# Feed-forward rows turned by VectorE and DMA instead of TensorE, and two steps of the attention rows moved to GpSimd

## What is computed

```python
x = X
q, k, v = xpos(norm(x) @ W_Q), xpos(norm(x) @ W_K, down), norm(x) @ W_V
p = softmax(q @ k.T) * 0.9 ** abs(n - m)          # n, m: row and key
x = x + p @ v
def fp4(x):                                       # blocks of 16 along the row
    scale = maximum(max(abs(block)) / 6, 1e-12)
    return grid(block / scale) * scale            # 0, .5, 1, 1.5, 2, 3, 4, 6
z = fp4(norm(x))
h = silu(z @ fp4(w_gate).T) * (z @ fp4(w_up).T)   # 704 wide
out = x + fp4(h) @ fp4(w_down).T
```

## Time and profile before

| | |
|---|---|
| median of 3 runs | 2549.67 us (2548.38 to 2549.73) |
| span of the profiled execution | 2546.6 us |
| PE, PEld busy | 2518.4, 2290.0 us |
| DVE, ACT, POOL busy | 2140.9, 1489.8, 1816.8 us |
| granted TensorE clock | 0.999 of 2.4 GHz |
| DMA, mean over the span | 80 GB/s |

### The profile page before, as it was taken

One profiled execution on the slowest core, in us unless ns is written; L12 is line 12 of the kernel. 1 busy time (PEld: TensorE's weight loads), 2 busy tenths in 40 slices (PEclk: granted clock), 3 DMA queues, 4 the chain that ended last, 5 costly groups with the idle time before them and its releaser, 6 DMA issues.

```text
span 2546.6 us, 51904 instructions
## 1 busy us (share of the span) xinstructions
PE 2518.4 (99%) x16160; PEld 2290.0 (90%) x16160; DVE 2140.9 (84%) x4759; ACT 1489.8 (59%) x2966; POOL 1816.8 (71%) x1929
## 2 busy tenths in 40 slices
PE   8999999999999999999999999999999999999997
PEld 7888879999999999999999999999999999999996
DVE  8999878888878888888888888888888888888886
ACT  5766565656555655566565656565556655555654
POOL 6999956667767676667766776677666776677665
PEclk9999999999999999999999999999999999999999
DMA  8878511122111311131112111131113111211110
GB/s 285 302 271 299 186 50 30 34 86 66 38 40 45 107 37 42 34 106 42 42 34 91 62 38 40 45 107 39 42 34 106 41 42 34 95 58 38 40 38 22
DMA packets 163473, 203.27 MB, mean 80 GB/s; under 512 B 15184, under 2 KB 116752, under 8 KB 163216
## 3 DMA queue, kind: packets, MB, share of 16 engines
q1 hardware_dynamic: 163216, 200.01, 24.1%
HBM read 103.42 MB, written 77.59 MB: 71 GB/s over the span
## 4 chain that ended last, share of the span: by engine, by line
PE 85%; POOL 0%; DVE 0%; issue 0%; ACT 0%; POOLq 0%
PE score L516 27%; PE acc L655 19%; PE ring L516 19%; PE acc L516 9%; PE ring L622 6%; PE ring L675 3%; PE acc L697 1%; PE ring L613 1%; DVE hT L1226 0%; POOL probs L998 0%; ACT probs L823 0%; ACT hT L793 0%; POOL h_buf L1019 0%; POOL xv L1004 0%; POOL h_buf L1013 0%
## 5 line engine op out<-in xcount | busy, mean ns | idle before, releaser
L516 PE MATMUL score<-keys,q_st 128*128 128x512 f32 x3072 | 733.7, 394 | 3.0 <-ACT probs L823 2.6
L516 PEld LDWEIGHTS score<-keys,q_st 128*128 128x128 f32 x3072 | 567.0, 188 | 117.8 <-issue 3.0
L998 POOL TENSOR_TENSOR probs<-probs,decay 128x512 f32<-128x512 f32 (+3 forms) x416 | 450.7, 1097 | 197.5 <-ACT probs L823 197.5
L655 PE MATMUL acc<-vals,pT 128*128 128x256 f32 x3984 | 554.6, 286 | 0.8 <-DVE pT L1226 0.8
L516 PE MATMUL ring<-w_gu,xqT 128*128 128x512 f32 (+1 forms) x2304 | 509.1, 374 | 0.0
L655 PEld LDWEIGHTS acc<-vals,pT 128*128 128x128 f32 x3984 | 498.1, 189 | 7.3 <-DVE pT L1226 2.0
L516 PEld LDWEIGHTS ring<-w_gu,xqT 128*128 128x128 f32 x2304 | 419.0, 188 | 63.6 <-DVE xqT L1226 0.4
L793 ACT ACTIVATE xqT<-ring 128x256 fp32r<-128x256 f32 x128 | 49.3, 385 | 706.9 <-PE ring L613 706.9
L1239 DVE TENSOR_REDUCE smax<-score 128x1 f32<-128x1024 f32 x256 | 312.8, 1222 | 95.6 <-PE score L516 94.1
L1226 DVE TENSOR_TENSOR pT<-ring,pT 128x512 fp32r<-128x512 f32 (+3 forms) x432 | 248.7, 600 | 66.7 <-ACT pT L793 65.5
L1004 POOL TENSOR_TENSOR xv<-xv,xe 128x256 f32<-128x256 f32 x128 | 94.4, 737 | 269.1 <-DVE xv L1079 269.1
(11 more groups left out here) (133 smaller groups left out, 4470.0 us busy)
## 6 DMA issues: line engine op xcount, KB each, us to landing
k_dram<-keys SPq DMA_DIRECT2D x56, 512.0 KB, 4.5
keys<-k_dram SPq DMA_DIRECT2D x56, 512.0 KB, 7.3
edge<-vals SPq DMA_DIRECT2D x288, 64.0 KB, 2.1
q_raw<-q_dram SPq DMA_DIRECT2D x129, 128.0 KB, 2.6
x_in<-X SPq DMA_DIRECT2D x32, 512.0 KB, 4.5
q_dram<-q_stage SPq DMA_DIRECT2D x32, 512.0 KB, 5.4
x_res<-X SPq DMA_DIRECT2D x128, 128.0 KB, 2.1
out<-x_res SPq DMA_DIRECT2D x128, 128.0 KB, 1.7
```

What stands on the lines that cost most here:

```text
L516: mm = pe.matmul(dst, stat(a, k), mov(m, k), start=i == 0, stop=ends and i == n - 1)
L655: mm = pe.matmul(pv_out, pT[g % 2][:, a, j * P:(j + 1) * P], edge[places[m]][:] if kb in edges else vals[m][:, kb, :], start=i == 0, stop= ...
L998: op = pool.tensor_tensor(probs[:, k0:k1], probs[:, k0:k1], decay[:, off + k0:off + k1], ALU.mult)
```

## The change

- TensorE's `h_transposed` is gone, with its two slots of the ring. In its place VectorE turns the 24 blocks of 32x32 of each quarter (`h_turned_blocks`, one `dve.transpose` over 128x768), for tile s-4, after the lower halves of the pieces. SP writes the turned tile to DRAM in one DMA, waits for it, and reads it back in four DMAs of 32 partitions each into `hqT` (`rows_turned`), which puts the quarters in their places. The next step ScalarE copies the upper half of all 768 columns from `hqT`, after pieces 0 and 1, and VectorE makes the lower half (`h_lower`) after its pieces 0 and 1 and ahead of the second maximum. Both now read SBUF.
- `hq` is one buffer instead of two; the other half holds the turned rows. So GpSimd's rounding of h waits for VectorE's transpose of the tile before.
- In the chain of xv GpSimd makes the block scales (`x_block_scales`, after all decay products) and, after `values`, the factor `rstd2 * xrs` and the product with xv (`x_normalised`). VectorE keeps the maxima, the reciprocal and the rounding. VectorE waits twice more for GpSimd (`x_scaled`, `x_normed`).
- Tile 0's blocks are cut 4, 4 instead of 2, 3, 3. With two pieces, GpSimd's `rstd` follows both decay products.
- On SP, `rows_turned` stands after `load_q`, ahead of values, edges, store and residual load.

```diff
@@ groups
-    size = CT if 0 < t < T - 1 else CT - 1
+    size = CT if t < T - 1 else CT - 1
@@ plan_slots
-            for h in range(2):
-                if g == min(max(len(gs) - LATER, 0) + h, max(len(gs), 1) - 1) and has(s - LAG):
-                    take("hT", s - LAG, h)
@@ buffers
-        hq = [hq_buf[:, i * FT:(i + 1) * FT] for i in range(2)]
+        hq, h_turn = (hq_buf[:, i * FT:(i + 1) * FT] for i in range(2))
+        hqT = [sb(f"hqT{i}", [P, CT, HK * QUAD]) for i in range(2)]
+        h_dram = nc.dram_tensor("h_dram", (2, P, CT, HK * QUAD), F32, kind="Internal").ap()
@@ SyncE
+            def rows_turned(j, t):
+
+                g, i = j * T + t, t % 2
+                sp.wait_ge(h_turned, g + 1)
+                passed()
+                if t > 1 or not isinstance(j, int) or j:
+                    sp.wait_ge(h_split, g - 1)
+                    passed()
+                sp.dma_start(h_dram[i], h_turn.rearrange("p (c r) -> p c r", c=CT)).then_inc(turn_out, 16)
+                sp.wait_ge(turn_out, (g + 1) * 16)
+                for c in range(CT):
+                    sp.dma_start(hqT[i][c * QUAD:(c + 1) * QUAD, :, :], h_dram[i, :, c, :].rearrange("(a i) r -> i a r", a=CT)).then_inc(hqT_back[i], 16)
@@ step
+                if s >= TURNED or not is_first:
+                    rows_turned(j, s - TURNED)
@@ ScalarE, h_transposed, now after pieces 0 and 1
-                    for h, n in enumerate((CT, HK - CT)):
-                        upper(hT[0][:, h * CT:h * CT + n, :].rearrange("p k t -> p (k t)"),
-                              bank(at, "hT", t, h)[:, 0:n * P], at, "hT", t, h)
+                    act.wait_ge(hqT_back[t % 2], halves(at, t) * CT * 16)
+                    if has(at, t - 1):
+                        act.wait_ge(dn_done, tile(at, t))
+                    act.activation(chunks(hT[0][:]), quads(hqT[t % 2][:]), ACT.Copy).then_inc(h_upper, 1)
@@ GpSimd
+            def x_block_scales(at, t):
+                if has(at, t):
+                    g = tile(at, t)
+                    pool.wait_ge(x_maxed, g + 1)
+                    pool.sem_inc(pool_passed, 1)
+                    pool.tensor_scalar(xs[:], xam[:], rstd6[:, 0:1], 1e-12, ALU.mult, ALU.max).then_inc(x_scaled, 1)
+
+            def x_normalised(at, t):
+                if has(at, t):
+                    g = tile(at, t)
+                    pool.wait_ge(ln2_rstd, g + 1)
+                    pool.wait_ge(x_inverse, g + 1)
+                    pool.tensor_tensor(xrs[:], xrs[:], rstd2[:, 0:1].to_broadcast([P, XB]), ALU.mult).then_inc(x_factor, 1)
+                    pool.wait_ge(x_factor, g + 1)
+                    pool.tensor_tensor(blocks(xv[:]), blocks(xv[:]), spread(xrs[:], XB), ALU.mult).then_inc(x_normed, 1)
@@ step
+                x_block_scales(at, s - 1)
                 for h in values_at(at, s):
                     values(at, h)
+                x_normalised(at, s - 1)
                 x_quantised(at, s - 1)
@@ VectorE
+            def h_turned_blocks(at, t):
+                if has(at, t):
+                    dve.wait_ge(hq_ready, tile(at, t) + 1)
+                    if has(at, t - 1):
+                        dve.wait_ge(turn_out, tile(at, t) * 16)
+                    dve.transpose(h_turn.rearrange("p (c k j) -> p k c j", c=CT, j=QUAD), hq.rearrange("p (k c i) -> p k c i", c=CT, i=QUAD)).then_inc(h_turned, 1)
+
+            def h_lower(at, t):
+                if has(at, t):
+                    dve.wait_ge(h_upper, tile(at, t) + 1)
+                    dve.tensor_tensor(chunks(hT[1][:]), quads(hqT[t % 2][:]), chunks(hT[0][:]).bitcast(F32), ALU.subtract).then_inc(h_split, 1)
@@ step
                 attend(at, s - 1, range(min(n, 2)))
+                h_lower(at, s - LAG)
                 maxima(at, s, 1)
...
                 attend(at, s - 1, range(2, n))
-                for h in range(2):
-                    h_transposed(at, s - LAG, h)
+                h_turned_blocks(at, s - TURNED)
```

More of the change, by code:

```diff
@@ L46 @@
 RING = 3
-XR, LAG, LATER = 8, 5, 3
+XR, LAG, TURNED = 8, 5, 4
+QUAD = 32
 W_SLOTS = 3
@@ L502, in _ @@
                 step(B - 1, s, False, False)
-            for t in range(T - LAG, T):
-                store(B - 1, t)
+            for s in range(T, T + LAG):
+                if s - TURNED < T:
+                    rows_turned(B - 1, s - TURNED)
+                store(B - 1, s - LAG)
             for i in range(XR):
@@ L687, in down @@
                 if has(at, t):
-                    copied(at, "hT", t, 1)
+                    pe.wait_ge(h_split, tile(at, t) + 1)
                     if t == 0 and at[2] is first_plan:
@@ L1306, in x_levels @@
                     return
-                then, wait, count = chain(xq_step, (tile(at, t) + 1) * NSTEP_XQ - 3)
-                wait()
-                dve.wait_ge(ln2_rstd, tile(at, t) + 1)
-                then(dve.scalar_tensor_tensor(blocks(xv[:]), blocks(xv[:]), rstd2[:, 0:1], spread(xrs[:], XB), ALU.mult, ALU.mult))
+                then, wait, count = chain(xq_step, tile(at, t) * NSTEP_XQ)
                 meanwhile(0)
-                wait()
+                dve.wait_ge(x_normed, tile(at, t) + 1)
                 levels(then, wait, xv[:], xe[:], xg_ready, meanwhile)
-                assert count() == 3
+                assert count() == NSTEP_XQ
             def h_made(at, t, p):
```

59 lines of the change are left out of this document (23 added, 36 removed).

## The result

The changed kernel takes **2696.2 us** (median; 2694.1 to 2700.0), the kernel before 2549.6 beside it: a ratio of 1.058 (95% interval 1.056 to 1.059), 146.5 us more. I had forecast 2609, at most 2662: the sign was right, the size was not.

What follows compares the result with a forecast made beforehand. TensorE was taken as the bound, by only 0.4 us. Per batch -6.9 + 6.4 + 5.0 = +4.5, eight times 36, plus 14 and 9 = +59: 2609 us; own range 2570 to 2650, wider range 2490 to 2662.

Steps and rivals of the forecast that it cites:

- rounding of h: VectorE's rounding of h, held at its old length of 900 ns beside an idle GpSimd; no cost in the sum.
- six transposes: Six transposes a pass leave TensorE, taken as 0.65 us a pass, 83 us if all of it arrived.
- x part: Scale and product of xv in GpSimd's queue make the next first maximum late in some passes: 5.0 us a batch.
- collision of `h_lower` (c): `h_lower` waits for GpSimd's subtraction ahead of the second maximum: 0.33 us, or 0.7 in some passes; 6.4 us a batch.
- borders: At batch borders the turned rows' DMAs queue behind the next batch's keys: 2 us, 7 times, 14 us.
- end: At the kernel's end the DMA round trip stands open once, about 11 us for 2 of the old path: 9 us.
- signs named ahead: TensorE idle 0.5 to 2 us a pass before piece 2, `h_lower` above 1.2 us, VectorE waiting on GpSimd, late first maximum.
- The transpose, 0.9: VectorE's block transpose of 128x768, not in the trace, taken as 0.9 us; bounds near 0.5 and 1.8.
- Rival 4: VectorE's transpose takes 1.8 us, ahead of `var`: 65 us more, 2674 us; chance 0.09.
- rival 1: TensorE keeps the bound and the gain arrives, c near 0, late passes covered: 2505 to 2520 us; chance 0.33.
- Rival 2: Gain and losses cancel within 0.2%, c near 0, late passes as worked out: 2549 us; chance 0.07.
- Rival 5: The DMA round trip is over 1 us too slow in every pass: 2700 us; chance 0.08.

Runs made afterwards that it cites:

- mixed: turn_wait with `h_lower` ahead of the first maximum; TensorE transposes h for one tile in 16 and the last four; tile 0 in three pieces: 2534.2 us.
- One_input: The changed kernel with `h_lower` as an instruction with one input of the same size, the lower half of h left out of the result: 2615.2 us.
- x_only: The kernel before with only the scale and product of the attention rows moved to GpSimd; hT still goes through TensorE: 2574.3 us.
- turn_only: The changed kernel with the scale and product of the attention rows back on VectorE, all else kept: 2620.6 us.
- turn_wait: turn_only with GpSimd's decay products waiting until VectorE has rounded h: 2599.3 us.
- x_early_wait: x_early with GpSimd's decay products also waiting until VectorE has rounded h: 2646.4 us.
- x_early: The changed kernel with GpSimd's scale directly behind `rstd` and its product with xv ahead of the values' work: 2673.4 us.

## Why the prediction was right in sign and wrong in size

**The step that failed.** The sum took the terms of a pass one by one and held everything the change doesn't touch at its old length and place. The largest term so missed is the rounding of h, put at nothing: it went from 900 to 1552 ns, and keeping GpSimd from it gives back 41 us. By the experiments and the ledger, what was forecast and what was found, in us of the kernel:

| term | forecast | found |
|---|---|---|
| six transposes | -83 | -46 |
| rounding of h beside the decays | 0 | 41 |
| x part, on top of the turned rows | 40 | 76 |
| collision of `h_lower` (c) | 51 | 81 |
| borders | 14 | 29 |
| end | 9 | 17 |

(The forecast's 59 also holds 28 for TensorE's stands without c.) The terms found overlap: each comes from a kernel in which the others are still there, and with the 28 they add up to 226 where 146 were measured. So they rank, but don't divide, the loss.

**The signs named ahead mostly came.** TensorE stands ahead of later pieces, released by the pT split, in 14 of 16 passes; the second maximum waits for scores in 3 passes instead of 112 (of the 34.5 us left, 32 are the first maximum's); VectorE waits 1.5 us in the mean for the scale; `h_lower` averages above 1.2 us. Two came otherwise: the wait for the product is 1.15 us in passes with `values` but also 0.36 in the others, and the first maximum is late behind more passes than 5, 7 and 10, by 1.0 us or more also behind 1, 3 and 14.

**Six transposes, 0.65 us a pass: too much.** I took the weight loads' busy time. In passes in which TensorE stands for nothing (5, 7, 9 and 10 of mixed) a pass is 0.35 to 0.37 us shorter than before, so all six are worth 0.36, 46 us in the kernel and not 83. The loads' busy time, most of which overlaps matmuls, was the wrong price; the forecast's own reading by starts, 0.5, was nearer and still too high. This makes the true gain per batch, before any loss, 5.8 instead of 10.4 us.

**The transpose, 0.9: right.** 969 ns; the estimate of about 1 us from the Trainium skill (VectorE: DVE Perf Modes, The three transpose paths) was nearer still, with some luck: in proportion to the width, 311 ns would make 1.87 us, and the step from there to 1 us was not written down. Rival 4 did not occur.

**The wait c of `h_lower`, 0.33 us and 0.7: right in kind, too small.** It was worked out from one pass on time, in which the call comes just ahead of the subtraction's end. The instruction took 0.66 us more than the one with one input, on average over all passes, where my c averages 0.43. The working held the call's time fixed while its neighbours moved: in a late pass the call meets more of the subtraction (in the pass shown it begins 0.63 us behind it and takes 1.88). One_input gives back 81 us, where c was to cost 6.4 x 8 = 51; as the rounding of h fell with it, not all of the 81 is c.

**The rounding of h, cost nothing: missed.** The earlier trace rows has it at 900 ns and the prediction used it only as a yardstick "beside an idle GpSimd". The change itself brings GpSimd beside it: without ScalarE's hT copies ahead of the exponential, the decay products begin earlier. In pass 7 they began at S+13.67 and the rounding at S+12.89 before, so it was done in time; now they begin at S+11.83, and the rounding still at S+12.89. 0.65 us a pass (1552 less 900), of which the waiting decays give back 41 us in the changed kernel and 21 without the x part. I had counted the decays' earlier start only as a help (rival 1).

**GpSimd in the chain of x, 5.0 us a batch: too much alone, too little together.** The lateness itself was forecast well: in x_only the first maximum comes 1.2, 1.4, 1.8 and 1.2 us after S+3.03 behind passes 1, 5, 7 and 10, against 0.9, 1.3, 1.5 and 1.1 forecast (though 0.6, 0.2, 0.5 and 0.0 of that were there before the change). (The 1.5 has a slip of 0.37 us in it: `rstd` was begun at the end of `var`, but the earlier trace rows has 0.37 between them.) But lateness is not time lost. Eight times 5.0 is 40; x_only costs 25, on top of the turned rows 76. I summed per pass and let the next pass absorb the lateness; that held for the kernel before, whose VectorE has that time, and not for one in which the transpose, the slower `h_lower` and the slower rounding have eaten it. The passes that lose most are 2, 6 and 15 (3.1, 2.8 and 2.6 us), each behind one named as late.

**The border, 2 us: half of it.** 4.2 us in the changed kernel, 5.0 in turn_only. The out transfer lands after 7.6 to 8.8 us in the changed kernel and after 8.5 to 10.2 in turn_wait, where I had 8, but the four back transfers and the edge rows come behind it in one queue. **The end, 9:** the wait for hT grew by 9.4, as forecast, but the whole stretch by 17.0, and with the last four tiles on the old path (mixed) 13.6 of it come back. The number was right for the one wait and too small for the end.

**TensorE's clock: no term of the sum.** The granted clock over the span is 0.990 against 0.999; 0.9% of 2692 us is 24 us, and this is an upper bound, since the mean counts the time in which TensorE stands. Over half of it lies in the last 75 us, at 0.80 (0.97 in the last 57 before). The products of gate and up and of down, the same in number, are busy 9.7 and 6.7 us longer. This is part of the lengths above, not on top of them.

**Rivals.** Rival 1 (the gain arrives) needed c near 0 and late passes covered; mixed shows what it looks like, but with a gain of 15 us, not 30 to 45, because the transposes are worth less. Rival 2 (no change) did not occur either. Rival 5 (the round trip too slow in each pass) did not occur: ScalarE waits for the rows only in 10 passes, all at borders or at the end.

## What stays open

The x part costs 25 us alone and 76 on the turned rows. With the decays' wait and its own better order it still costs 47 (2646.4 less 2599.3). The slower `h_lower` (1557 ns in x_early_wait against 1305 in turn_wait, 32 us if the pass follows one for one) would be more than the 22 that lie between 47 and 25, but this was not separated from the two hand-overs. Neither was the mask over xv, slowed beside the values' product in x_early_wait as in x_early (788 ns in the mean against 424 in turn_wait, 47 us of VectorE's time): no run has the better order without this collision. And what the uncollided `h_lower` would give on top of mixed was not tried.

## What to carry over

Before moving work between VectorE and GpSimd, write down for each VectorE instruction with two SBUF inputs, and for mask steps with one, which GpSimd instruction will run beside it after the change, the untouched ones too; the two-input ones here went from 0.9 to 1.6 us. Price a removed TensorE instruction by how much earlier the next starts, not by its weight load's busy time, and take even that (0.5 us here) as a bound: 0.36 came. A DMA round trip that is covered in the steady state is to be looked at where a bulk load shares the queue and the engines; here it paid to leave the one tile of 16 at that place on its old path.

## What the runs showed of the hardware beyond what I had expected

A wait added on GpSimd made the kernel 41 us faster, by keeping its products from running beside VectorE's rounding (893 against 1552 ns). A VectorE mask step with a single tensor input is slowed as well: 527 ns alone, 2064 where GpSimd's 2.0 us subtraction runs beside it; and the mask over xv 294 alone, 1367 beside GpSimd's product of the values. VectorE's block transpose takes 969 ns whether GpSimd is busy beside it (103 cases) or not (25). A 6 us stand of TensorE was followed by some 3 us of work at a granted clock of 0.50. And a 384 KB transfer that takes 2.3 us in the median took 8.5 to 10.2 behind transfers of 512 KB.
